# A softplus evaluated in one step, a new order of TensorE's work in a half pair, and a front that starts later in a chunk

## The reference, cut to what matters

```python
xz = x @ W_in.T                                  # x_val and z, 256 channels each
xv = conv1d(x_val, conv_w, causal, 4 taps) + conv_b
x_val = silu(xv)
dt = softplus(x[:, :, :64] @ W_dt.T + b_dt)      # the step size
Bm, Cm = x @ W_B.T, x @ W_C.T                    # 16 states each
h = exp(dt * A) * h + (dt * x_val) * Bm          # one step per token, 256 x 16 states
y = (h @ Cm) * silu(z)
out = y @ W_out.T
```

## Time and profile before

| | before |
|---|---|
| median of 3 runs | 755.2 us |
| lowest run | 753.4 us |
| the profiled execution | 755.35 us |
| its span, first to last instruction | 753.3 us |
| PE busy | 544.0 us (72%) |
| DVE busy | 445.1 us (59%) |
| ACT busy | 373.3 us (50%) |
| POOL busy | 380.1 us (50%) |
| mean granted TensorE clock | 0.871 of 2.4 GHz |

### The profile page before, as it was taken

One profiled execution on the slowest core, in us unless ns is written; L12 is line 12 of the kernel. 1 busy time (PEld: TensorE's weight loads), 2 busy tenths in 40 slices (PEclk: granted clock), 3 DMA queues, 4 the chain that ended last, 5 costly groups with the idle time before them and its releaser, 6 DMA issues.

```text
span 753.3 us, 7011 instructions
## 1 busy us (share of the span) xinstructions
PE 544.0 (72%) x2400; PEld 366.6 (49%) x2400; DVE 445.1 (59%) x731; ACT 373.3 (50%) x521; POOL 380.1 (50%) x232
## 2 busy tenths in 40 slices
PE   4678666596979883689874968787768669067673
PEld 3456444354868752576552646554456523023232
DVE  6467877524222111398835767683488766487972
ACT  2324322254453573867864756487756628223211
POOL 2138577424000036166739756464956655756461
PEclk9679889688989996889988889999979889697897
DMA  9300000000000020011001100010111111011100
GB/s 342 111 1 0 1 1 0 1 0 1 1 0 2 1 95 19 1 41 44 29 9 49 57 28 31 33 36 24 50 42 51 34 42 59 28 56 56 43 0 14
DMA packets 12563, 26.94 MB, mean 36 GB/s; under 512 B 1968, under 2 KB 7472, under 8 KB 12272
## 3 DMA queue, kind: packets, MB, share of 16 engines
q1 hardware_dynamic: 11952, 25.57, 10.0%
q10 hardware_dynamic: 576, 0.92, 0.4%
HBM read 25.31 MB, written 1.18 MB: 35 GB/s over the span
## 4 chain that ended last, share of the span: by engine, by line
PE 35%; DVE 29%; ACT 15%; POOL 12%; issue 8%; DMA 1%; ACTq 0%; DVEq 0%; POOLq 0%
PE pO L1164 9%; DVE Hs L720 8%; DVE pCT L709 5%; DVE S L614 3%; PE pY L1234 3%; PE pH L1152 3%; ACT dA L934 2%; PE pH L1154 2%; PE pH L1153 2%; ACT gel L922 2%; POOL Zev L359 2%; PE pY L1229 2%; DVE pH L613 2%; ACT ln_x L776 2%; ACT L934 2%
## 5 line engine op out<-in xcount | busy, mean ns | idle before, releaser
L1164 PEld LDWEIGHTS pO<-w_e,gel 128*128 128x128 f32 x1024 | 135.3, 203 | 18.4 <-issue 9.0
L1164 PE MATMUL pO<-w_e,gel 128*128 128x128 f32 x1024 | 136.7, 287 | 2.3 <-DVE X L690 2.3
L720 DVE TENSOR_TENSOR_SCAN Hs<-dA,HL,pCT 128x512 f32<-128x512 f32 x96 | 117.7, 1268 | 20.2 <-POOL Zev L359 18.6
L922 ACT ACTIVATE gel<-pH,b_e 128x512 f32<-128x512 f32 x128 | 85.8, 686 | 85.2 <-PE pH L1154 84.6
L709 DVE TENSOR_TENSOR pCT<-u,pB 128x1024 f32<-128x1024 f32 x64 | 78.3, 1223 | 51.2 <-PE pB L1217 50.4
L934 ACT ACTIVATE dA<-dt,a_neg 128x512 f32<-128x512 f32 x128 | 81.9, 711 | 53.0 <-DVE Hs L720 39.2
L359 POOL TENSOR_TENSOR Zev<-Hs,Crow 128x1024 f32<-128x1024 f32 x32 | 78.4, 2451 | 58.4 <-DVE Hs L720 52.5
L690 DVE SCALAR_TENSOR_TENSOR X<-pO,wts,X 128x128 f32<-128x128 f32 x128 | 36.0, 344 | 93.8 <-PE pO L1164 93.8
L1152 PE MATMUL pH<-h2h,w_e1h 128*128 128x512 f32 x128 | 64.3, 502 | 33.4 <-DVE wts L677 13.5
L359 POOL TENSOR_TENSOR Zod<-Hs,Crow 128x1024 f32<-128x1024 f32 x19 | 44.9, 2363 | 55.0 <-DVE Hs L720 55.0
L1217 PE MATMUL pB<-ST,sel 96*128 96x512 bf16 x64 | 27.1, 424 | 61.0 <-DVE pCT L709 60.9
(11 more groups left out here) (204 smaller groups left out, 1036.4 us busy)
## 6 DMA issues: line engine op xcount, KB each, us to landing
Crow<-c_rows SPq DMA_DIRECT2D x32, 512.0 KB, 3.7
w_e<-in_w_e SPq DMA_DIRECT2D x2, 2048.0 KB, 10.5
X<-in_x SPq DMA_DIRECT2D x4, 256.0 KB, 6.5
out<-outb SPq DMA_DIRECT2D x4, 256.0 KB, 4.4
S<-in_w_mod ACTq DMA_DIRECT2D x2, 384.0 KB, 4.5
w_cx<-in_conv_row SPq DMA_DIRECT2D x1, 512.0 KB, 9.2
w_f<-in_w_f SPq DMA_DIRECT2D x2, 128.0 KB, 5.4
b_e<-in_b_e SPq DMA_DIRECT2D x1, 256.0 KB, 13.6
```

Source lines behind the costliest of these rows:

```text
L720: vec.tensor_tensor_scan(Hs[:, 2 * o + d, 0:w], dA[:, 4 * (p % 2) + 2 * o + d, 0:w], pU[:, d, 0:w], HL[:, d, n:n + 1] if c else 0.0, ALU.m ...
L922: nc.scalar.activation(gel[:, n % NG, 0:w], pH[n % 2][:, 0:w], ACT.Gelu_apprx_tanh, bias=b_e1[:, NK * e + k:NK * e + k + 1]).then_inc(s["m ...
L1164: ins = mm(pO[:, j * P:(j + 1) * P], gel[:, n % NG, j * P:(j + 1) * P], w_e2[:, NK * (g % E) + k, :], start=(k == 0 and j == 0), stop=(k = ...
```

## The change

The step size is `ACT.Softplus` with the bias b_dt, straight from PSUM into `dt`: `soft`, `one`, the tiles `exd`, `lnd` and `wx`, and the addition on VectorE go. The front's stages stand two places later or more, and `rows` stands ahead of `dt_part`. Both halves of the convolution go through pH1, where the first one used pH0. `AHEAD` is 12. In a half pair, TensorE does the second `up` behind the first `down`.

```diff
-AHEAD = 13
+AHEAD = 12
...
                 if 0 <= front < NL:
-                    plan += [(8, "ln_stats", front), (9, "ln_apply", front), (9, "ln_turn", front, 1), (9, "dt_part", front),
-                             (10, "soft", front), (10, "x_part", front, 0), (11, "rows", front), (11, "one", front),
-                             (12, "x_part", front, 1), (14, "z_part", front), (14, "step", front)]
+                    plan += [(10, "ln_stats", front), (11, "ln_apply", front), (11, "ln_turn", front, 1), (12, "rows", front),
+                             (12, "dt_part", front), (12, "x_part", front, 0), (14, "x_part", front, 1),
+                             (14, "z_part", front), (15, "step", front)]
...
-                elif stage == "one":
...
-                    link(pool.tensor_scalar(wx_, exd_, 1.0, None, ALU.add))
-                    link(pool.tensor_scalar(wx_, wx_, -1.0, None, ALU.add))
-                    link(pool.tensor_tensor(wx_, wx_, exd_, ALU.subtract))
-                    pool.wait_ge(s["mam_ln"], c + 1)
-                    pool.tensor_tensor(lnd_, lnd_, wx_, ALU.subtract).then_inc(s["mam_l1"], 1)
...
             def step(c):
 
                 d_ = half_of(dt, c)
-                vec.wait_ge(s["mam_l1"], c + 1)
-                sig(vec.scalar_tensor_tensor(d_, d_, 0.0, lnd[:, :, 0:WIDTHS[c]], ALU.max, ALU.add), "mam_dt", c + 1)
+                vec.wait_ge(s["mam_dt"], 2 * c + 2)
                 vec.wait_ge(s["mam_xc"], 2 * c + 2)
...
-                nc.scalar.activation(xc[:, d, 0:w], pH[d][:, 0:w], ACT.Silu, bias=col(f"conv_b{d}")).then_inc(s["mam_xc"], 1)
+                nc.scalar.activation(xc[:, d, 0:w], pH1[:, 0:w], ACT.Silu, bias=col(f"conv_b{d}")).then_inc(s["mam_xc"], 1)
...
             def dt_part(c):
                 v_ = half_of(dt, c)
+                if c >= 2:
+                    act.wait_ge(s["mam_u"], c - 1)
                 for d in range(ND):
                     act.wait_ge(s["mam_dtp"], 2 * c + d + 1)
-                    nc.scalar.activation(exd[:, d, 0:WIDTHS[c]], pH[d][:, 0:WIDTHS[c]], ACT.Abs,
-                                         bias=col(f"b_dt{d}")).then_inc(s["mam_ab"], 1)
-                    nc.scalar.activation(v_[:, d, :], pH[d][:, 0:WIDTHS[c]], ACT.Identity,
-                                         bias=col(f"b_dt{d}")).then_inc(s["mam_v"], 1)
+                    nc.scalar.activation(v_[:, d, :], pH[d][:, 0:WIDTHS[c]], ACT.Softplus,
+                                         bias=col(f"b_dt{d}")).then_inc(s["mam_dt"], 1)
...
-            def soft(c):
-                exd_, lnd_ = exd[:, :, 0:WIDTHS[c]], lnd[:, :, 0:WIDTHS[c]]
-                act.wait_ge(s["mam_ab"], 2 * c + 2)
-                nc.scalar.activation(exd_, exd_, ACT.Exp, scale=-1.0).then_inc(s["mam_ex"], 1)
-                act.wait_ge(s["mam_ex"], c + 1)
-                nc.scalar.activation(lnd_, exd_, ACT.Ln, bias=1.0).then_inc(s["mam_ln"], 1)
...
                 if g < NL * E:
                     up(g, 2 * o)
-                    up(g, 2 * o + 1)
                 if 0 <= 2 * p + o + 1 < NL * NS:
                     row_b(2 * p + o + 1)
                 if 0 < g <= NL * E:
                     down(g - 1, 2 * o)
+                if g < NL * E:
+                    up(g, 2 * o + 1)
                 if o and p > 0:
                     total(p - 1)
...
-                use(d, "mam_xc", 2 * c + d + 1)
+                use(1, "mam_xc", 2 * c + d + 1)
                 for k in range(TAPS):
-                    ins = mm(pH[d][:, 0:w], w_cx[:, d, k, :], h3T[:, k:k + w], start=(k == 0), stop=(k == TAPS - 1))
+                    ins = mm(pH1[:, 0:w], w_cx[:, d, k, :], h3T[:, k:k + w], start=(k == 0), stop=(k == TAPS - 1))
```

More of the change, by code:

```diff
@@ L149, in build @@
         h2l = sb("h2l", [P, 2, TC], F32R)
+        cmp_ = sb("cmp", [P, TC])[:, :].rearrange("p (k t i j) -> p k t i j", k=2, t=NJ, i=E)
         h3T = sb("h3T", [P, HALO + TC])
@@ L164, in build @@
         BCf = sb("BCf", [96, 2, TC])
-        exd = sb("exd", [P, ND, TC])
-        lnd = sb("lnd", [P, ND, TC])
-        y2 = exd
-        wx = sb("wx", [P, ND, TC])
+        y2 = sb("y2", [P, ND, TC])
         gz = sb("gz", [P, 2 * ND, TC])
@@ L172, in build @@
         u = sb("u", [P, 2 * ND, TC])
-        cmp_ = lnd[:, 1, :].rearrange("p (k t i j) -> p k t i j", k=2, t=NJ, i=E)
-        P1 = wx[0:96, 0, 0:TC // 2].bitcast(BF16)
+        P1 = y2[0:96, 0, 0:TC // 2].bitcast(BF16)
         ST = sb("ST", [96, 2, TC], BF16)
@@ L222, in build @@
             moe_rt moe_lg moe_ex moe_w moe_wt moe_wts moe_bias moe_xb moe_h moe_g moe_g2 moe_acc
-            mam_hist mam_xp mam_zp mam_gz mam_dtp mam_bc mam_bcs mam_xc mam_v mam_ab mam_ex mam_ln mam_l1 mam_dt mam_u
+            mam_hist mam_xp mam_zp mam_gz mam_dtp mam_bc mam_bcs mam_xc mam_dt mam_u
             mam_st0 mam_st mam_cd mam_bB mam_ub mam_dA mam_sc mam_z mam_zs mam_y mam_y2 mam_o mam_x
@@ L440, in _ @@
                     pool.wait_ge(s["mam_st0"], c + 1)
+                    pool.wait_ge(s["ln_rstd"], L[0])
                     for name, count in done.items():
@@ L456, in _ @@
                                        ALU.subtract).then_inc(s["h2_lo"], 1)
-                elif stage == "one":
-                    w = WIDTHS[c]
-                    exd_, lnd_, wx_ = exd[:, :, 0:w], lnd[:, :, 0:w], wx[:, :, 0:w]
-                    pool.wait_ge(s["mam_ex"], c + 1)
-                    link(pool.tensor_scalar(wx_, exd_, 1.0, None, ALU.add))
-                    link(pool.tensor_scalar(wx_, wx_, -1.0, None, ALU.add))
-                    link(pool.tensor_tensor(wx_, wx_, exd_, ALU.subtract))
-                    pool.wait_ge(s["mam_ln"], c + 1)
-                    pool.tensor_tensor(lnd_, lnd_, wx_, ALU.subtract).then_inc(s["mam_l1"], 1)
-                    pool.wait_ge(s["mam_l1"], c + 1)
                 elif stage == "fft":
@@ L928, in decays @@
                 if k == 0:
-                    act.wait_ge(s["mam_dt"], c + 1)
+                    act.wait_ge(s["mam_dt"], 2 * c + 2)
                 if p >= 2:
@@ L950, in _ @@
                     half(c, *k)
-                elif stage in ("route", "turn", "x_part", "rows", "dt_part", "z_part", "soft"):
+                elif stage in ("route", "turn", "x_part", "rows", "dt_part", "z_part"):
                     {"route": route, "turn": turn, "x_part": x_part, "rows": rows, "dt_part": dt_part,
-                     "z_part": z_part, "soft": soft}[stage](c, *k)
+                     "z_part": z_part}[stage](c, *k)
         @block.tensor
@@ L1200, in dt_part @@
                 for d in range(ND):
-                    use(d, "mam_v", 2 * c + d + 1)
+                    use(d, "mam_dt", 2 * c + d + 1)
                     mm(pH[d][:, 0:WIDTHS[c]], w_dt[:, d, :], h4T[:, 0:WIDTHS[c]], start=True, stop=True).then_inc(s["mam_dtp"], 1)
```

## The result

| | before | after |
|---|---|---|
| median | 754.7 us (4 runs) | 712.05 us (4 runs) |
| ratio to before, 95% interval | | 0.9439 [0.9417, 0.9461] |
| profiled execution, its span | 755.35, 753.3 us | 712.84, 710.8 us |
| PE / DVE / ACT / POOL busy | 544.0 / 445.1 / 373.3 / 380.1 us | 534.3 / 434.3 / 354.0 / 337.8 us |
| mean granted TensorE clock | 0.871 | 0.897 |

Ratios leave out a run that lies far off the others: here one of the four of before, at 2780 us, and later one of the four with the matmuls repeated, at 742.7 us. The change is faster by 5.6%, and the forecast of 709 was 3 us low.

What follows compares the result with a forecast made beforehand. Fronts, where scans wait behind POOL's roundings, and a joint-pair ring of 8.80 us were taken to bound the kernel. Terms -12 - 11.5 - 15 - 15.5 + 9.7 + 3 - 6.5 + 1 = -46.8 took 755.35 to 708.5, forecast 709 us, range 694 to 731.

Steps and rivals of the forecast that it cites:

- POOL's stage and softplus: In each chunk's front, POOL loses 10.5 us and VectorE's 2.70 us addition goes; softplus is one pass of 0.7 us.
- the rival with 1.4 us or a second load: Softplus passes of 1.4 us, or one more load each: 6 to 10 us more, 717 us; chance 0.07.
- the 721: Estimate in us if 1.38 us of draining follows each table load, 4 us more per in-scan front; not adopted.
- The fronts: Stretches before chunks 1, 2, 3 shorten by 12, 11.5 and 15 us, that before chunk 0 by 15.5.
- the rival in which they give back half: ScalarE's run and two convolution halves replace POOL; in-scan fronts gain only 5 or 6 us each: 731 us; chance 0.17.
- The order: TensorE's new order in half pairs: +9.7 us in joint and router pairs, +3 with experts alone.
- the ring: Joint pairs' 8.80 us cycle from u times row through TensorE to scans; second `up` inside adds 0.7 us, 7.7 over 11.
- the cover of `moe_acc`: In pairs with experts alone, one `up` instead of two covers the wait: +0.7 us in 7 pairs, +3 net.
- The rival that the order costs nothing: Ups and waits slide so the ring never closes and 12.7 us of stalls go: 696 us; chance 0.15.
- Experts alone: Pairs running only experts were to take 7.2 us each.
- AHEAD 12: One pair with an expert alone goes, -6.5 us; pair 19 becomes a joint pair, +1.
- the rival that ends slower: TensorE's added waits in joint pairs drop its clock to 0.5, up to 68 us lost: 777 us; chance 0.03.

Runs made afterwards that it cites:

- the matmuls repeated: Changed kernel with the step size's matmuls in `dt_part` issued four times (first bank) and three times (second), same result: 0.9464 of the kernel before.
- the run with the old order: Changed kernel with TensorE's half pair back to up, up, B row, down, down, all else as changed: 0.9156 of the kernel before, 692.5 us.
- half 1 alone: Changed kernel with the new order in half 1 of each pair only, half 0 with both ups first as before: 0.9337 of the kernel before.
- the `down` alone: Changed kernel with half pairs in the order up, down, up, B row, (sum,) down: 0.9370 of the kernel before.
- own banks: Changed kernel with the old order and the convolution halves in pH0 and pH1 again: 0.9103 of the kernel before, 686.5 us.

## Why the prediction was right, and where it was off

*POOL's stage and softplus.* Right. Softplus is one pass at 0.64 us, the rival with 1.4 us or a second load is out, and POOL's stage is off the chain. The trace shows the load at 1.28 us and the softplus 0.01 us behind it (372.29, 373.58): the 1.38 us of draining that the Trainium skill gives ("ScalarE: Activation LUTs", "What ACT_TABLE_LOAD costs") stands in no row here either, and the 721 that the prediction works out with it was not reached. The run with POOL's work put back shows that the dependence was most of the price.

*The fronts.* Chunk 1's came out at 64.8 for 64.7 laid out, and the rival in which they give back half is out. In the rows the half clock cost less than laid out (convolution 6.07 for 3.6: 2.5 us of the 4) and other waits took the rest. Here is the **mis-sized term**: the last front gave 12.3 for 15, chunk 2's 10.2 for 11.5, and what lies before chunk 0 17.8 for 19. With the 0.2 of chunk 1 these are 5.4 us, the whole miss in the table above, 41.4 for 46.8. In the last front the layout counted pair 20 as one without an expert (7.5 us, the two `moe_acc` apart), and it took 9.6; u took 3.22, since POOL's instruction stood first. The medians miss by 3 us only, since the first expert started 1.1 us earlier in the changed kernel's profile, and its execution, 712.84, was 0.8 above the median; that these two helped is luck.

*The order.* The sum had +12.7, of it 9.7 in the stretches between the fronts, and these show +10.7 with AHEAD's 1, as laid out; the +3 with experts alone is 2.7 by the run with the old order. But taking the order away gives 18.6 us by the profiles and 21 by the ratios. About 5 us of it lie inside the fronts (76.6, 69.4 and 54.2 against 73.3, 67.5 and 54.4 over the five pairs), where I had laid out the new order and booked the result to the front. The rest had the right sum for a partly wrong reason: half 1 alone, where the prediction had all of the 9.7, gives some 5 in these stretches. Pairs 10 and 18 lose nothing and I had 0.7 for each, while pairs 3, 11 and 19, with `weigh` and `fft`, lose 2.1 to 2.9 and I had 1 for each of two. The working knew only two things, the ring and the cover of `moe_acc`; ScalarE, made late by half 0, was missing. That errors offset each other there is luck. The rival that the order costs nothing is out.

*Experts alone.* `moe_acc` follows `moe_acc` after 7.2 us (241.78 to 249.01, 249.01 to 256.16), as forecast.

*AHEAD 12.* -5.5 forecast, -2 by the ratios (not told from nothing), -5.5 from the first expert on: not contradicted.

*The bank.* "Cost nothing more" is contradicted by the profiles, with 6.7 us; the ratios have some 4, within their intervals.

*The clock.* In the plain pairs it stayed 1.00 (337.40 to 346.60), so the rival that ends slower is out. It fell in the fronts, as laid out, but not there alone: in the kernel before it was also 0.50 from 316.6 to 326.8 us (pairs 0 and 1) and from 596.5 to 603.3 (pair 19), and in the changed kernel the mean over pair 11 is 0.82.

## What to carry to other kernels

When instructions are reordered on one engine, follow the ring that limits the pair and then the second engine that is fed: an instruction moved behind a wait costs nothing in the ring and may still make the next engine late for every stage that needs its buffer. Price each part of a combined change against the kernel without it; here one part (the softplus) brought 7.7%, another (the order) took nearly 3% back, and the total looked like a success. If a stage is removed, ask whether its time or its place in the dependence was the price, since 37 us of POOL's work put back without the dependence cost some 4.

## What the runs showed of the hardware

- Softplus with a bias from PSUM, 128x512 in float32, is one pass of 0.69 us (two take 1.27) with one table load of 1.28 us ahead of it.
- The wait ahead of a front's first convolution half goes with its granted clock but doesn't settle it. In the eight traces with the later front unspread, the bank pH1 for both halves and no repeated matmuls, TensorE waited 1.4 to 2.2 us there; 30 of the 32 halves took 5.2 to 6.7 us at a mean clock of 0.54 to 0.71, and two (the first fronts of the runs with POOL's work and with the `down` alone) took 3.67 at full clock behind the same 2.2 us. With own banks, behind 1.6 us, three of four took 3.67 and one 5.26; with the matmuls repeated, behind 0.9 us, all four took 3.67.
- Getting the full clock back for the convolution (7 us less in all) did not make the kernel faster, when it was bought with more matmuls in front.
- VectorE's u and POOL's instructions on 128x1024 held each other up whole, and whichever started first went first. Where POOL's was under way, u ended 1.08 us behind its end, in every such front of the traces, and so took 1.55 to 3.39 us. Where u started first (the three fronts of the run with softplus alone, the last of the run with POOL's work) it took 1.22 or 1.23 us, and POOL's, 0.03 to 0.06 us later, took 3.39 to 3.41 instead of 2.35.
